# Full attention with its step loop written out, a step's order of products, value groups and jobs laid out anew, and the same PSUM banks

## What is computed

```python
qh, kh, vh = proj(q, W_q, b_q), proj(k, W_k, b_k), proj(v, W_v, b_v)   # 16 heads of 16 features
scores = jnp.einsum('bhqd,bhkd->bhqk', qh, kh) / jnp.sqrt(jnp.float32(D_K))
scores = jnp.where(m == 0, jnp.float32(NEG_INF), scores)
attn = jax.nn.softmax(scores, axis=-1)
context = jnp.einsum('bhqk,bhkd->bhqd', attn, vh)
```

## Time and profile before

| what | value |
|---|---|
| timed runs, median | 5217.95 us |
| profiled execution, span | 5209.4 us, mean granted clock 0.944 |
| TensorE (PE) busy | 4733.7 us, 91% |
| VectorE (DVE) busy | 3852.0 us, 74% |
| ScalarE (ACT) busy | 2767.8 us, 53% |
| line 1185, maxima, DVE | 2025.7 us, 3392 instructions |
| line 1161, exponentials, ACT | 1744.9 us, 3328 instructions |
| steps of full attention | from about 1565 to 3950 us |

### The profile page before, as it was taken

How to read it: one execution, slowest core, us unless ns; L and a number is a source line. 1 busy time by engine, 2 the same in 40 slices (tenths; PEclk the granted TensorE clock), 3 DMA queues, 4 the chain that set the end, 5 groups by cost and what they waited for, 6 DMA issues and landing times. The chain is left out here.

```text
span 5209.4 us, 96256 instructions
## 1 busy us (share of the span) xinstructions
PE 4733.7 (91%) x28783; PEld 2782.8 (53%) x28784; DVE 3852.0 (74%) x7481; ACT 2767.8 (53%) x5099; POOL 1289.2 (25%) x996
## 2 busy tenths in 40 slices
PE   8979997999579999999999999999997803999999
PEld 4546664777244444444444444444444602888887
DVE  7766665664758888887888888888894723877886
ACT  2225552222327777877777777777783101444443
POOL 5630001221631101110110110111001264554544
PEclk9989998999779999999999999999997756999999
DMA  7766663220872332443334334333314654333332
GB/s 216 222 183 166 161 167 114 82 83 33 269 167 48 67 77 58 76 78 70 56 65 80 61 71 78 74 52 72 60 35 111 182 174 122 61 63 81 59 62 37
DMA packets 326842, 519.92 MB, mean 100 GB/s; under 512 B 50000, under 2 KB 242863, under 8 KB 324192
## 3 DMA queue, kind: packets, MB, share of 16 engines
q1 hardware_dynamic: 294816, 461.48, 36.4%
q0 software_dynamic: 28208, 51.82, 4.7%
q10 hardware_dynamic: 3360, 0.98, 0.1%
HBM read 254.97 MB, written 179.55 MB: 83 GB/s over the span
## 5 line engine op out<-in xcount | busy, mean ns | idle before, releaser
L1185 DVE TENSOR_REDUCE full_peak<-full_item 128x1 f32<-128x512 f32 (+2 forms) x3392 | 2025.7, 654 | 339.9 <-PE full_item L1247 323.9
L1161 ACT ACTIVATE full_prob<-full_score 128x512 f32<-128x512 f32 (+1 forms) x3328 | 1744.9, 601 | 401.3 <-PE full_score L1257 386.1
L1247 PE MATMUL full_item<-full_kst,full_qst 49*128 49x512 f32 (+1 forms) x4096 | 1171.0, 403 | 8.5 <-DMA full_kst<-full_high 5.2
L1257 PE MATMUL full_score<-full_qst,full_kst 51*128 51x512 f32 (+1 forms) x3328 | 1028.8, 434 | 8.7 <-issue 7.6
L1247 PEld LDWEIGHTS full_item<-full_kst,full_qst 49*128 49x128 f32 x4096 | 618.8, 188 | 603.6 <-DVE full_peak L1185 538.6
L1267 PE MATMUL full_value<-full_prob,full_vaug 128*17 128x512 f32 x6656 | 879.2, 600 | 0.6 <-ACT full_prob L1161 0.4
L1257 PEld LDWEIGHTS full_score<-full_qst,full_kst 51*128 51x128 f32 (+1 forms) x3328 | 504.9, 182 | 371.7 <-ACT full_prob L1161 294.4
L1100 POOL TENSOR_TENSOR full_low<-full_low,full_keep 128x1601 f32<-128x1601 f32 x32 | 116.0, 3625 | 2020.0 <-ACT full_low L1135 2020.0
L2550 ACT ACTIVATE moe_h<-moe_hbank,moe_b 128x512 f32<-128x512 f32 (+1 forms) x320 | 200.0, 625 | 450.5 <-PE moe_hbank L2643 445.4
L2653 PE MATMUL moe_ybank<-moe_w_both,moe_h_high 128*128 128x512 f32 x1088 | 386.6, 399 | 0.1
L754 DVE TENSOR_REDUCE win_peak<-win_item 128x2 f32<-128x384 f32 x512 | 262.2, 552 | 124.1 <-PE win_item L794 117.1
(11 more groups left out here) (274 smaller groups left out, 7278.9 us busy)
## 6 DMA issues: line engine op xcount, KB each, us to landing
full_kst<-full_high SPq DMA_DIRECT2D x256, 200.1 KB
full_ctxT<-in_ctxT SPq DMA_DIRECT2D x16, 1601.0 KB, 9.2
full_kst<-full_low SPq DMA_DIRECT2D x128, 200.1 KB
win_qst<-scratch_q SPq DMA_DIRECT2D x384, 64.0 KB, 2.7
full_qst<-scratch_q SPq DMA_DIRECT2D x384, 64.0 KB
scratch_xbuf<-ctxp_zero POOLq DMA_DIRECT2D x17, 1032.0 KB, 7.7
moe_x<-scratch_xbuf SPq DMA_DIRECT2D x32, 516.0 KB, 3.8
scratch_attn<-win_raw SPq DMA_DIRECT2D x64, 256.0 KB, 2.1
```

The lines of the kernel that those rows point to most:

```text
L1161: nc.scalar.activation(prob_of(s, h, kt)[0:rows, :], score[score_bank(u)][0:rows, :], ACT.Exp, scale=SCALE).then_inc(score_read, 1)
L1185: nc.vector.tensor_reduce(peak[s.par][:, hq:hq + len(qts), c], src, AX, ALU.max).then_inc(item_read, 1)
L1247: ins = nc.tensor.matmul(ps[:, at:at + z - a], qst[s.slot][rows, h // 2, qt * P:(qt + 1) * P].bitcast(F32R), kst[s.slot][rows, h // 2, a:z ...
L1257: nc.tensor.matmul(score[score_bank(u)][0:z - a, :], kst[s.slot][rows, h // 2, a:z].bitcast(F32R), qst[s.slot][rows, h // 2, :].bitcast(F3 ...
```

## The change

The loop over steps becomes 64 written-out steps. `STEP_ORDER` and `ITEM_HALVES` get new values; the number of each letter stays the same. The number of item banks becomes a name and stays 3. Bank numbers are now worked out from the running number of the unit or item, since every step's number is a constant.

```diff
 def windows_by_batch(eng, body):
-    for k in range(8):
-        body(Step(0, k), k == 0, 2)
-    with eng.Fori(1, BATCH // 4) as j:
-        for k in range(16):
-            body(Step(j * 4 - 2, k), False, 2)
-    for left in (7, 6, 5, 4, 3, 2, 1, 0):
-        body(Step(0, STEPS - 1 - left), False, min(left, 2))
+    for k in range(STEPS):
+        body(Step(0, k), k == 0, min(STEPS - 1 - k, 2))
...
-    SCORE_BANKS = 4
+    SCORE_BANKS, ITEM_BANKS = 4, 3
...
-    STEP_ORDER = ("SSISIVISSIISJSIISISJISISSIVISISSISVSSIIIJIISSISVSISISISVIISSISVSIISSSIIIVISIISVISSIIVSISISIVISSISIJI"
-                  "SISSISIVISISSIVSIISSIVI")
-    ITEM_HALVES = ("010101010101101010110111001111101111110110111101010111")
+    STEP_ORDER = ("SISSISIVISSSIIJIISSIJISSIIVIISSSIVISISSSIVISSISSSIISISIVISSISIVISSIVSIISSIVISSSIISVIIJSIIIJSIISSIVII"
+                  "SSSISIVIISSSIVISISSSIIV")
+    ITEM_HALVES = "110110101010100110101001010101010011001010110010101101"
...
-        at = len(prologue) + PER_WINDOW * (s.k % 3)
-        return [(*it, base + n, (at + n) % 3) for n, it in enumerate(items)]
+        return [(*it, base + n, (base + n) % ITEM_BANKS) for n, it in enumerate(items)]
...
-    def score_bank(u):
-        return (len(ALL_JOBS) + u) % SCORE_BANKS
+    def score_bank(s, u):
+        return (first_unit(s) + u) % SCORE_BANKS
...
             def item(kind, s, j, number, bank):
-                at_least(pe, item_read, number - 2)
+                at_least(pe, item_read, number - ITEM_BANKS + 1)
```

More of the change, by code:

```diff
@@ L932, in window_items @@
         base = len(prologue) + PER_WINDOW * s.n
-        at = len(prologue) + PER_WINDOW * (s.k % 3)
-        return [(*it, base + n, (at + n) % 3) for n, it in enumerate(items)]
+        return [(*it, base + n, (base + n) % ITEM_BANKS) for n, it in enumerate(items)]
     def turn_number(s):
-        if isinstance(s.n, int) and s.n == 0:
+        if s.n == 0:
             return NMAX
@@ L943, in full_attention @@
                 + [("max", Step(0, 1), j) for j in range(HEAD)])
-    prologue = [(*it, n, n % 3) for n, it in enumerate(prologue)]
-    assert PER_WINDOW % 3 == 0
+    prologue = [(*it, n, n % ITEM_BANKS) for n, it in enumerate(prologue)]
     def place(h, qt):
@@ L953, in batch_par @@
         return s.turn % 2 if isinstance(s.turn, int) else s.k // 4 % 2
-    def score_bank(u):
-        return (len(ALL_JOBS) + u) % SCORE_BANKS
-    assert UNITS % SCORE_BANKS == 0 and EXPS % SCORE_BANKS == 0
+    def score_bank(s, u):
+        return (first_unit(s) + u) % SCORE_BANKS
     with ExitStack() as ctx:
@@ L964, in full_attention @@
         score = [ps(f"score{i}", [P, 512]) for i in range(SCORE_BANKS)]
-        item_bank = [ps(f"item{i}", [P, 512]) for i in range(3)]
+        item_bank = [ps(f"item{i}", [P, 512]) for i in range(ITEM_BANKS)]
         value = ps("value", [P, SQ])
@@ L1154, in window @@
                     if kind == "job":
-                        read_job(base + u, score_bank(u), JOBS[s.slot][e], s.turn + 1, 1 - batch_par(s))
+                        read_job(base + u, score_bank(s, u), JOBS[s.slot][e], s.turn + 1, 1 - batch_par(s))
                         continue
@@ L1160, in window @@
                     at_least(act, value_done, KT * s.n + kt - PROB_BUFS + 1)
-                    nc.scalar.activation(prob_of(s, h, kt)[0:rows, :], score[score_bank(u)][0:rows, :], ACT.Exp,
+                    nc.scalar.activation(prob_of(s, h, kt)[0:rows, :], score[score_bank(s, u)][0:rows, :], ACT.Exp,
                                          scale=SCALE).then_inc(score_read, 1)
@@ L1256, in scores @@
                 rows = slice(64 * (h % 2), 64 * (h % 2) + ROWS)
-                nc.tensor.matmul(score[score_bank(u)][0:z - a, :], kst[s.slot][rows, h // 2, a:z].bitcast(F32R),
+                nc.tensor.matmul(score[score_bank(s, u)][0:z - a, :], kst[s.slot][rows, h // 2, a:z].bitcast(F32R),
                                  qst[s.slot][rows, h // 2, :].bitcast(F32R), start=True, stop=True).then_inc(score_full, 1)
@@ L1286, in window @@
                     elif token == "J" and busy(s):
-                        job(first_unit(s) + u, score_bank(u), JOBS[s.slot][units(s)[u][1]], s.turn + 1, 1 - batch_par(s))
+                        job(first_unit(s) + u, score_bank(s, u), JOBS[s.slot][units(s)[u][1]], s.turn + 1, 1 - batch_par(s))
                         u += 1
```

## The result

The changed kernel takes 5287.01 us (median of 4 runs, 5284.14 to 5287.67), the kernel before 5218.82 (4 runs): a ratio of 1.0127, 95% interval 1.0113 to 1.0142. It is slower by 68 us, 1.3%. 5279 was predicted, in a range of 5208 to 5318.

What follows compares the result with a forecast made beforehand. TensorE sets the pace at 37.3 us a step, VectorE having 13% to spare. Span 5209.4 - 19.4 (loop) + 78 (waits less pairing) + 3 (last steps) = 5271; plus 8.5 to the timed median, 5279 us, range 5208 to 5318.

Steps and rivals of the forecast that it cites:

- the price list: TensorE: 0.20 us a run plus 0.23 a slot (one product or an opposite-half pair); VectorE: 0.60 us an item.
- N7: Run of 13 products, six of them items, before a step's fifth V: 2.93 us instead of 1.82, +1.11.
- N17: New order's five-slot run whose fourth item waits for a bank: 1.73 us instead of 1.36, +0.37.
- N3: A run of four slots in the new order, priced at 1.12 us.
- N12: A run of the new order with small products of about 0.11 us, estimated at 0.70 us.
- Part 1: Loop written out: TensorE's stalls at the two jumps back go, 19.4 us less.
- Part 2: Better pairing in an ordinary step's runs: 17.50 us instead of 18.20, a gain of 0.70 us a step.
- Part 3: Waits for item banks added by the new order, in N7, N17 and around N14: 2.00 us a step.
- N14: Three-item run behind a job: +0.88 us in slots 0 and 2, 0 in slot 1, +0.32 in slot 3.
- Part 4: Last four steps, without jobs, where banks already bind: new order's longer runs cost 3 us, bounds 0 and 6.
- The rival of the falling clock: N7's wait halves TensorE's clock for 3.4 us every step, costing 1.7 us more a step: 5381 us, chance 0.03.
- The other rivals: Waits hidden, 5154 us (0.12); only N7 costs, 5224 us (0.12); written-out code short of instructions, 5298 us (0.03).

Runs made afterwards that it cites:

- the halved runs: Changed kernel, and the old order with loop written out, each with maxima over half the keys and exponentials over half the queries: 5173.68 and 5160.16 us.
- the first experiment: Changed kernel with old STEP_ORDER and ITEM_HALVES set back, so only the loop is written out: 5200.76 us, ratio 0.9965 to the kernel before.

## Why the prediction was right, step by step

- *What bounds it, and the price list.* Right. The new runs were forecast from the earlier trace rows and measured within a few hundredths: N7 2.93 and 2.96, N17 1.73 and 1.70, N3 1.12 and 1.11, N11 1.12 and 1.13. N12, my estimate of 0.70, took 0.57.
- *Part 1, the loop.* Right in its cause. Its 19.4 us of stalls are those of the trace that I read; a second profile of the same kernel has 16.7. Against these two profiles the steps from the first to the 59th copy gained 22 and 20 us by the loop alone.
- *Part 2, slots.* The gain was forecast as 0.70 us a step; it is 0.65 by the halved runs. Summed over an ordinary step's runs, the old order written out takes 18.21 us (18.20 in the prediction) and the new one 19.36, of which 1.97 are the waits below: 17.39 remain (17.50 in the prediction), so 0.82 by this count. A cost that the prediction had at nothing goes against it: the last job of a step takes 0.09 us more in every slot (0.59 instead of 0.50 for the small key job). It is no wait for a bank, since it stays at 0.59 with both readers halved; what changed is that a score now stands behind it and not the turn. Why this costs 0.09 stays open.
- *Part 3, waits.* 2.00 us a step forecast. Measured: N7 +1.14, N17 +0.35, N14 +0.78 in key slots, 0 in slot 1 and +0.36 in slot 3, 0.48 on average: 1.97. 1.97 + 0.09 - 0.82 is 1.24, and the steps agree. The net, from the first to the 59th copy of the values, is 72.0 us between the first experiment (2162.0) and the changed kernel (2234.0), 1.24 for each of 58 steps; 1.30 was forecast.
- *Part 4, the last four steps.* The term that was mis-sized. 3 us forecast; in the two profiles compared it was 18.3 us (180.9 against 162.6 from the 59th copy to the last). Of this the trace that I read held 9 to 13 us of luck, since the old order took 175.7 in the kernel's second profile and 171.9 with the loop written out; the other 5 to 9 would be the order's. No run shows them apart. The working had a slip too: the three steps of the earlier trace rows were taken as free of jobs, but the first of them holds the last two value jobs (3792.6 and 3809.4), so the 31.0 us don't hold for it.
- *The rival of the falling clock.* Wrong where I put it: N7's wait left the clock at 1.00 in all 60 steps. Right elsewhere: in the steps without jobs. There N2 to N4 and N12 to N14 grow together into runs that last 5.0 and 4.3 us at VectorE's pace, and towards the end of each the clock falls:

```profile
3873.20:3880.00 6.80, 6.39 (x34) 3.08 (x30) 5.34 (x10) 4.61 (x9) 0.00 (x0) 0.79 0.21 67
3897.20:3903.40 6.20, 5.56 (x29) 1.98 (x25) 4.82 (x11) 2.87 (x6) 0.00 (x0) 0.81 0.00 0
3914.30:3921.00 6.70, 6.39 (x34) 3.09 (x30) 5.46 (x10) 4.72 (x10) 0.00 (x0) 0.78 0.10 39
```

 The old order has runs of 4.44 us there, and they don't decide it: the clock fell at each of the three in the kernel's second profile and with the loop written out, and at none of them in the profile that the prediction was read from. Nor does it take waits on items: in all three profiles of the old order it also fell in a run of nine scores alone, 10 us or more behind the last item.

 The Trainium skill ("TensorE: Matmul & The Clock Gate", A second HAM failure mode: psum-queue depth-cycling) says that frequent short idle times of TensorE between groups of matmuls, where PSUM banks are cycled through, make the clock go back and forth. The trace agrees in the last steps, with 0.78 to 0.81 in the rows above, and does not in N7, with 1.00.
- *The other rivals.* The waits were not hidden, N7 was not the only place, and the written-out code ran through: TensorE has no gap over 1 us up to the 59th copy.
- *The sum.* 5279 forecast, 5287 measured; that they lie 8 apart is in part luck. In spans it was 5271 against 5285.8, 15 apart: the last four steps were 15 too cheap, the stages behind took 5 more with unchanged code and the stretch ahead of the first copy 1 more; against that the step was 0.06 us too dear, 3 in all, and the loop gave 3 more. The 8.5 us from span to time made up for half of this: in every run since, a run's time lies 1.8 us above its own span, so the other 6.7 were the luck of the profiled execution, which had run faster than the median.

What stays open: what decides, from one execution to the next, whether the clock falls in the last steps, and why the stages behind this one take 1257 to 1264 us with unchanged code; the 1264.0 of the changed kernel are also those with the most half clock, 344 us against 334 to 343 in the others.

## What to carry to other kernels

An engine at 100% can be made better and still lose: count for each burst how many buffers it asks for, how long the reader takes to free one, and whether the reader was idle just before. N7 found its three item banks free and still took 1.14 us more than its slots, because its last items could only go at the reader's pace. Look at one profile's best stretch with suspicion; a second profile of the unchanged kernel would have shown that its tail at full clock was chance.

## What was not expected of the hardware

- The granted clock held at 1.00 while TensorE waited 1.14 us in all inside one run of 3 us, 60 times, and fell in runs of 4.3 to 5.0 us whose pairs stood 0.60 us apart instead of 0.23. In runs of 4.44 us of the kernel before it held in one profile and fell in the other.
- Writing the loop out also took 0.2 us from one step in four, beside the stalls at the jumps.
- A halved maximum (256 instead of 512 columns) still left a round of 1.0 us from an item's start to its free bank (2125.77 to 2126.82), 0.57 of it before VectorE begins.
